# Late steps of a fused attention and expert layer: where products, expert additions, gathers and the turn of c stand

## What is computed

```python
x = L0_attn_x                                    # (8, 512, 512) fp32
xn = layernorm(x)
out = x + attention(xn, Wq, Wk, Wv, Wo) + experts(xn, gate_w, expert_w, expert_b)

def attention(x, Wq, Wk, Wv, Wo):                # 16 heads of 32, causal
    q, k, v = (x @ W.T split into heads for W in (Wq, Wk, Wv))
    q, k = rope(q), rope(k)
    return (softmax(mask(q @ k.T / sqrt(32))) @ v, heads joined) @ Wo.T

def experts(x, gate_w, expert_w, expert_b):      # 8 experts, 2 per token, no capacity limit
    top_vals, top_idx = top_k(x @ gate_w.T, 2)
    w = softmax(top_vals)
    return sum over the two chosen of w * (x @ expert_w[e].T + expert_b[e])
```

## Time and profile before

| | |
|---|---|
| median of 3 runs | 986.21 us (985.04 to 988.06) |
| profiled execution | 989.46 us, span of its instructions 987.7 us |
| TensorE matmuls busy | 919.4 us (93%) |
| VectorE busy | 739.2 us (75%) |
| GpSimd busy | 561.2 us (57%) |
| ScalarE busy | 437.1 us (44%) |
| early steps | about 77 to 430 us |
| experts | about 436 to 651 us |
| late steps | about 651 to 988 us |

### The profile page before, as it was taken

How to read it: one execution, slowest core, us unless ns; L and a number is a source line. 1 busy time by engine, 2 the same in 40 slices (tenths; PEclk the granted TensorE clock), 3 DMA queues, 4 the chain that set the end, 5 groups by cost and what they waited for, 6 DMA issues and landing times.

```text
span 987.7 us, 18755 instructions
## 1 busy us (share of the span) xinstructions
PE 919.4 (93%) x6589; PEld 450.7 (46%) x6589; DVE 739.2 (75%) x1327; ACT 437.1 (44%) x711; POOL 561.2 (57%) x553
## 2 busy tenths in 40 slices
PE   2899898899899999989999999998999999999887
PEld 1344344344354544545555555553444444444333
DVE  7888988798789899954444444467788888788865
ACT  5267867757755443431111221133434454334432
POOL 1545677575675446663333333238877888778741
PEclk9999999999999999999999999999999999999999
DMA  6365678598677443396655555455555564555431
GB/s 242 107 225 183 192 268 312 170 331 288 193 261 287 138 163 127 115 335 193 204 175 176 176 177 171 161 193 171 184 176 182 186 196 140 156 184 175 162 109 54
DMA packets 107963, 188.63 MB, mean 191 GB/s; under 512 B 11872, under 2 KB 65248, under 8 KB 102624
## 3 DMA queue, kind: packets, MB, share of 16 engines
q1 hardware_dynamic: 97072, 152.03, 44.4%
q0 software_dynamic: 10800, 35.40, 12.7%
HBM read 117.13 MB, written 70.25 MB: 190 GB/s over the span
## 4 chain that ended last, share of the span: by engine, by line
PE 65%; DVE 14%; DMA 7%; POOL 5%; ACT 4%; issue 3%; SPq 1%; DVEq 0%; ACTq 0%; POOLq 0%
PE psum L952 19%; PE psum L1037 10%; PE psum L1061 6%; PE psum L1000 5%; PE psum L987 5%; PE psum L1003 4%; PE psum L969 4%; PE psum L1046 4%; PE psum L929 4%; DVE top L1486 4%; DMA c_rows<-c_turn 2%; DMA sum_sb<-x 2%; PE psum L971 2%; ACT pT L764 1%; DMA x_blk<-xn_rows 1%
## 5 line engine op out<-in xcount | busy, mean ns | idle before, releaser
L764 ACT ACTIVATE pT<-psum,factors 128x512 f32<-128x512 f32 (+1 forms) x352 | 218.2, 642 | 247.2 <-PE psum L987 238.2
L1486 DVE TENSOR_REDUCE top<-psum 128x1 f32<-128x384 f32 (+3 forms) x352 | 209.9, 634 | 20.8 <-PE psum L971 19.9
L1037 PE MATMUL psum<-xT,w_att 128*128 128x512 f16 x768 | 196.5, 381 | 6.9 <-DVE xT L1437 4.7
L952 PE MATMUL psum<-w_exp,x_gT 128*128 x852 | 195.3, 379 | 0.6 <-DVE x_gT L1442 0.6
L610 POOL DMA_INDIRECT x_g<-xn_rows,tok_of x71 | 67.3, 948 | 131.8 <-PE psum L929 129.5
L969 PE MATMUL psum<-k_stack,q_stack 96*128 96x384 f16 (+3 forms) x512 | 126.6, 300 | 14.3 <-DVE top L1486 13.2
L987 PE MATMUL psum<-q_stack,k_stack 98*128 98x256 f16 (+3 forms) x512 | 128.4, 303 | 7.4 <-ACT pT L764 4.5
L1442 DVE TENSOR_TENSOR x_gT<-psum,x_gT 128x512 f16<-128x512 f32 x71 | 49.0, 692 | 104.4 <-ACT x_gT L788 85.5
L952 PEld LDWEIGHTS psum<-w_exp,x_gT 128*128 128x128 f16 x852 | 83.3, 98 | 85.6 <-issue 0.9
L788 ACT ACTIVATE x_gT<-psum 128x512 f16<-128x512 f32 x71 | 42.3, 597 | 170.0 <-PE psum L929 167.5
L600 POOL TENSOR_TENSOR o_hl<-o_sb,o_hl 128x512 f16<-128x512 f32 x31 | 36.5, 1177 | 129.9 <-ACT o_hl L778 128.7
(11 more groups left out here) (175 smaller groups left out, 1296.3 us busy)
## 6 DMA issues: line engine op xcount, KB each, us to landing
y_rows<-y_sb SPq DMA_DIRECT2D x71, 256.0 KB
w_in<-w_all SPq DMA_DIRECT2D x12, 1024.0 KB, 11.4
q_stack<-qk_rows SPq DMA_DIRECT2D x96, 128.0 KB
k_stack<-qk_rows SPq DMA_DIRECT2D x96, 128.0 KB
x_in<-x SPq DMA_DIRECT2D x8, 1024.0 KB, 9.5
qk_rows<-q_hl SPq DMA_DIRECT2D x32, 256.0 KB
qk_rows<-k_hl SPq DMA_DIRECT2D x32, 256.0 KB
xn_rows<-x_in SPq DMA_DIRECT2D x8, 1024.0 KB, 5.1
```

Of the source, the lines that this page charges most:

```text
L764: act.activation(p_of(j, h, heads), banks[BANK_T + (NT_ * n + k) % 2][:, 0:W], ACT.Exp, scale=factors[:, 0:1]).then_inc(exp_done, 1)
L952: now = pe.matmul(banks[s % 4], x_gT[s % 4][:, xp * C + c, :], w_exp[:, bass.ds(e, 1), wp, c, :].rearrange("p e d -> p (e d)"), start=n == ...
L1037: now = pe.matmul(bank, w_att[:, what, wp, c, g * P:(g + 1) * P], xT[b % 2][:, xp * C + c, :], start=at_pass == 0, stop=at_pass == 3 * C - 1)
L1486: return dve.tensor_reduce(out=top[:, h:h + heads, i], in_=banks[BANK_S + k % 2][:, 0:heads * W].rearrange("p (h t) -> p h t", h=heads), a ...
```

## The change

Nothing of the arithmetic changes. In early steps only the turn of c does: c_hl becomes the first 32 columns of a zeroed tile of 128 (c_wide), and the whole tile is turned, which writes 128 partitions instead of 32; the copy still takes 32. scores(m, 0) no longer waits for c_copied, only scores(m, 1) does, whose bank the turn uses.

In late steps
- TensorE does all four products of step n in step n+1 behind scores(n+2, 3), and turns c behind shifted_scores(n, 10) instead of ahead of unit 9;
- ScalarE copies c behind exps 9 instead of exps 8, so behind the high part of k; in step 28 the high part of q goes behind exps 6;
- VectorE adds the expert rows of step n (n above 16) between the maxima of units 2 and 3 and normalise_o, instead of at the end of the step; step 16's stay at its end;
- GpSimd in step 16 gathers the second tile of step 16 behind mask 1 instead of ahead of k's rope, and both tiles of step 17 behind mask 3 instead of behind mask 1.

```diff
--- before.py
+++ after.py
@@ -124,7 +124,8 @@
     top = at("top", [P, HG, J], F32)
     c_scale = at("c_scale", [P, HG * J], F32)
     c_f = at("c_f", [P, HG * J], F32)
-    c_hl = at("c_hl", [P, 2, HG * J], F16)
+    c_wide = at("c_wide", [P, P], F16)
+    c_hl = c_wide[:, 0:2 * HG * J].rearrange("p (f r) -> p f r", f=2)
     c_turn = at("c_turn", [2 * HG * J, P], F16)
     rden_few = at("rden_few", [P, S // HD], F32)
     w_att = at("w_att", [P, NQ, 2, C, D], F16)
@@ -637,8 +638,6 @@
                     gather_x(1)
                 if n + 3 < N:
                     low_qk(0, n + 3)
-                if n == N1:
-                    gather_y(late_tiles(N1)[1])
                 if n in (CHOOSE + 2, CHOOSE + 3):
                     mask(n, 1)
                 if n + 3 < N:
@@ -646,8 +645,8 @@
                 if n not in (CHOOSE + 2, CHOOSE + 3):
                     mask(n, 1)
                 if n == N1:
-                    gather_y(late_tiles(n + 1)[0])
-                if n >= N1 and n + 1 < N:
+                    gather_y(late_tiles(N1)[1])
+                elif N1 < n < N - 1:
                     gather_y(late_tiles(n + 1)[1])
                 if n + 3 < N:
                     low_qk(1, n + 3)
@@ -660,6 +659,9 @@
                 mask(n, 3)
                 if n in TURN_AT:
                     low_x(TURN_AT[n], 3)
+                if n == N1:
+                    for w in late_tiles(n + 1):
+                        gather_y(w)
 
             pool.wait_ge(trig_in, 16)
             rope(0, 0)
@@ -810,17 +812,19 @@
                 if n == N1:
                     for u in range(4):
                         act.wait_ge(y_stored[u], 16 * len(range(u, NTILE, 4)))
-                if n + 3 < N:
+                if n + G < N:
                     high_qk(0, n + 3)
                 exps(n, 5)
                 exps(n, 6)
+                if n + G == N:
+                    high_qk(0, n + 3)
                 if n - 1 in JOB_AT:
                     high_w(JOB_AT[n - 1])
                 exps(n, 7)
                 if n + G < N:
                     take_v(n + G, BANK_QV)
                 exps(n, 8)
-                if n + 1 < N:
+                if n < N1:
                     copy_c(n + 1)
                 if n + 3 < N:
                     high_qk(1, n + 3)
@@ -828,6 +832,8 @@
                     high_x(TURN_AT[n], 0)
                     high_x(TURN_AT[n], 1)
                 exps(n, 9)
+                if N1 <= n < N - 1:
+                    copy_c(n + 1)
                 exps(n, 10)
                 if n in TURN_AT:
                     high_x(TURN_AT[n], 2)
@@ -963,7 +969,7 @@
                     pe.wait_ge(k_stacked[u], 48 * (m // 3 + 1))
                 if k >= 2:
                     pe.wait_ge(max_done, NS * m + k - 1)
-                elif m:
+                elif k and m:
                     pe.wait_ge(c_copied, m)
                 for h in range(heads):
                     pe.matmul(bank[:, h * W:(h + 1) * W], q_stack[u][0:ROW_C, h0 + h, i * P:(i + 1) * P], k_stack[u][0:ROW_C, h0 + h, 0:W],
@@ -973,7 +979,7 @@
 
             def turn_c(m):
                 pe.wait_ge(c_made, m + 1)
-                pe.transpose(half(BANK_S + 1)[0:2 * HG * J, 0:P], c_hl[:].rearrange("p f r -> p (f r)"), ident16[:]).then_inc(c_turned, 1)
+                pe.transpose(half(BANK_S + 1)[:, 0:P], c_wide[:], ident16[:]).then_inc(c_turned, 1)
 
             def shifted_scores(n, k):
                 h0, heads, j = T_UNITS[k]
@@ -1096,8 +1102,8 @@
                     free_bank_out(n)
                     spread_max(JOB_AT[n - 1])
                 if n and n != N1:
-                    times_v(n - 1, 2)
-                    times_v(n - 1, 3)
+                    for j in range(0 if n > N1 else 2, J):
+                        times_v(n - 1, j)
                 if n in KEEP_AT:
                     free_bank_out(n)
                     if n - 1 in JOB_AT:
@@ -1189,15 +1195,17 @@
                     if n == G:
                         pe.wait_ge(w_lo_done, 4)
                     project_out(wo[0], BANK_KO, 0, 4)
-                if nxt:
+                if n < N1:
                     turn_c(n + 1)
                 shifted_scores(n, 9)
                 if wo:
                     project_out(wo[0], BANK_KO, 4, 8)
                 shifted_scores(n, 10)
-                if nxt:
+                if n < N1:
                     times_v(n, 0)
                     times_v(n, 1)
+                elif nxt:
+                    turn_c(n + 1)
                 else:
                     times_v_last(0, 1, 2)
                 if wo:
@@ -1561,6 +1569,9 @@
                 if nxt:
                     largest_score(n + 1, 2)
                     largest_score(n + 1, 3)
+                if n > N1:
+                    for w in late_tiles(n):
+                        add_experts(w)
                 if n - 1 in JOB_AT:
                     scale_of(JOB_AT[n - 1])
                 if n == 1:
@@ -1624,9 +1635,10 @@
                     spread_low(1, 0)
                     spread_low(1, 1)
                     experts_of_tiles()
-                for w in late_tiles(n):
+                for w in late_tiles(n) if n == N1 else []:
                     add_experts(w)
 
+            dve.memset(c_wide[:], 0.0)
             own.link(dve.memset(c_scale[:], 2.0 ** -LOG_C))
             for u in range(2):
                 dve.memset(k_stack[u][ROW_C:ROW_C + 2, :, :], -2.0 ** LOG_C).then_inc(ones_made, 1)
```

## The result

The changed kernel takes **993.49 us** (median of 6 runs, 987.81 to 996.95) beside 986.41 (6 runs) for the kernel before: ratio 1.0063, 95% interval 1.0043 to 1.0083. Forecast were 982.4, at most 987.4. It is slower by 7.1 us where 3.8 us less were expected. The other 2.6 are that before's profiled run lay 3 us above its own median and after's 0.5.

A forecast was written before the change was run, and what follows sets the result against it. TensorE's own stream was taken to bound steady late steps, with waits for VectorE in early ones. Terms -0.5 - 4.6 + 2.0 + 1.2 + 1.0 - 1.6 - 1.3 = -3.8 us: 986.21 to about 982.4, range 978.6 to 987.4.

The forecast's parts named there:

- Tile switches: TensorE, late steps: full-width turn saves 0.19 us, one group of products instead of two 0.23, together 0.42 per steady step.
- the steady step: Late steps 18 to 27: 20.8 us becomes about 20.38; with step 17, 0.42 saved in each, -4.6 us.
- rival A: Steady steps: late expert additions or the copy of c give the gain back, 986.9 us; chance 0.22.
- The c_wide tile at nothing: Start of the kernel: the memset of c_wide lies beside the first loads and costs nothing, without cover 0.1 us.
- First late steps: Steps 16 and 17: moved gathers make TensorE stand 5 to 6 us, costing +2.0 and +1.2; bounds -5 and +5.
- the clock: Step 17: a stand of 6 us may bring 3.4 us at half clock, losing 1.7; taken at 0.6, +1.0 us.
- Step 28: q's high part follows exps 6, so TensorE's 1.37 us wait goes; net -1.6 us, between -0.4 and -2.
- steps 29 and 30: Last steps: two switches and the wait for c (0.1 to 0.3) go, -0.65 us each.
- Early steps: Steps 0 to 15: the turn's saving is mostly swallowed by waits for VectorE; 0.5 us gained, between 0 and 2.
- the last step: Step 31 keeps its length; its expert rows go ahead of normalise_o with 1 us to spare.
- C: Steady steps: the second gather lands late, at 5.4 us costing 8.8, so slower at 991 us; chance 0.08.

The follow-up runs named there:

- a3: The kernel before with only the turn of c in full width, all places and waits as before: 986.88 us, ratio 1.0006.
- b1: The changed kernel with c turned in 32 columns again, at the changed place: 991.18 us, ratio 1.0045.
- c4: The changed kernel with VectorE's expert additions of all late steps at the end of the step, as before: 1005.12 us, ratio 1.0187.
- d3: The kernel before with 192 unused bytes per partition behind c_hl, nothing else changed: 990.75 us, ratio 1.0037.
- e1: The changed kernel with c_wide behind all other tiles and 64 bytes left where c_hl was, so other tiles keep their old addresses: 988.19 us, ratio 1.0016.
- c1: The changed kernel with step 16's second tile added in step 17 before normalise_o, and step 17's tiles at its end: 984.91 us, ratio 0.9980.
- e2: c1 with c_wide behind all other tiles, so that every other tile has its address of before: 980.6 us, ratio 0.9945.
- d4: The changed kernel itself measured once more, nothing altered: 993.72 us, ratio 1.0063.
- a4: The kernel before with only GpSimd's gathers moved as the change moves them: 987.39 us, ratio 1.0013.
- e3: The kernel before with 256 unused bytes per partition behind c_hl, nothing else changed: 986.63 us, ratio 1.0006.
- d2: The kernel before with c_wide and the full-width turn up to step 16 alone: 992.46 us, ratio 1.0054.
- d1: c1 with c turned in 32 columns up to step 16, the c_wide tile kept: 987.43 us, ratio 1.0011.
- c2: c1 with products, turn and copy of c of steps 28 to 30 and additions from step 29 as in the kernel before: 987.08 us, ratio 1.0006.

## Why the prediction was wrong, and where it was right

**Tile switches and the steady step: right.** Forecast 20.38 with a saving of 0.42; measured 20.36 and 0.45. The turn alone brought 0.20 to 0.21 (a3, b1; I had taken 0.19). Steps 18 to 27 brought 4.16 of the 4.2 that ten steps of 0.42 are. Copy and additions did fit, if by little: rival A didn't happen, and c4 shows that the experts' place is what pays for it.

**The c_wide tile at nothing: the step that failed.** I priced its memset and its columns, not its bytes. It is the largest term that was missing: 4.0 us by the pad alone (d3), 4.6 by giving the changed kernel the old layout (e1), 3.5 between c1 and e2, and 4.6 on average in the start of the late steps. The +3.62 that the first section left open is this, within what single traces scatter. I had looked only at the engines' instructions; a diff that changes a tile's size in a kernel that places tiles one behind another changes all addresses behind it. The Trainium skill (DMA: Bandwidth & Descriptors, How a descriptor splits into AXI transactions) has the rule that I passed over: a descriptor is split into transactions of 256 bytes that start at multiples of 256, and one that starts between them fetches the bytes ahead of it as well. The page speaks of reading, and the loads here are shifted on the side that is written. Estimates by this rule, in its beats of 32 bytes: a run of 512 bytes that starts 192 past a multiple takes 22 in place of 16, 1.38 times, and the packets of 512 bytes took about 1.27 times as long; a run of 1,024 takes 1.19 times as many, and the packets took 1.05. The 1024 packets of 256 bytes, stores of c_turn, test it the other way: c_turn starts 192 bytes past a multiple before and 128 past one in the shifted kernels, so the rule gives 12 beats in place of 14, 0.86, and they took 17.2 to 17.4 ns in place of 19.2 to 19.4, 0.90. So the trace agrees in direction for three sizes and roughly in size for two of them; it is not the whole account. That 256 bytes of pad cost nothing is what it says.

**First late steps: mechanism right, size short.** On the time scale of the kernel before, whose late steps start 3.62 earlier, TensorE's stand ended at 675.1 where I had 675.3, after 5.98 us where I had 5 to 6. Step 17 cost 1.5 more where I had 0.8 (1.2, less the 0.42 of its switches). The term that was mis-sized is **the clock**: I gave a possible stretch of 3.4 us the weight 0.6 and 1.0 us in all. It was 6.8 us long, in both profiled executions of this kernel (after, d4) and in the three others with a stand of about 6 us (b1, c4, e1), and right on the products: from the end of the stand to shifted_scores(17, 0) 7.86 us passed, where 5.4 were forecast. That is about 2.5 lost. Forecast for the two steps and the clock 3.8, measured 5.8.
What I left unsaid is that the stand needed both moves: a4 moves the gathers alone and steps 16 and 17 come out 0.4 shorter together. And c1 shows that its whole price hung on one tile's addition in VectorE's order: step 16 falls from 29.17 to 20.28.

**Step 28 right in part by luck, steps 29 and 30 wrong by the clock.** Step 28 gained 2.2 (forecast 1.6). But 1.5 of it is a stretch of half clock that the step has in the profile of before (21.71) and in d3 and e3, and not in a3, a4 and d2 (20.20 to 20.26), behind the same wait of 1.36 to 1.37. Steps 29 and 30 were to gain 0.65 each and lost 0.75 and 0.26: each has 3.4 us of half clock behind a stand of 1.57 to 1.92 for the maxima, and I had no term for it. Without the stretch step 30 takes 13.99, in a second profile of the same kernel (d4), and 0.62 less than before, as forecast; so the stretch costs 0.88 there. Step 29 has one in every profile of this order, so that its order and its clock can't be told apart. Before stands as long in these steps, here in step 29, and had no such stretch there, only the one of step 28:

```profile
932.57 0.34 PE L969 MATMUL psum<-k_stack,q_stack 96*128 96x384 f16 x1 [1.57 <-DVE top L1486]
```

So a stand of that length is not enough to foretell it. Nor is the one of 2.82 to 2.85 us for a mask in step 16 of the kernels with the old gathers and products: the clock falls in it or just behind it in a3, d2 and e3, and not in before and d3. What else is needed stays open.

**Early steps: no gain to be seen.** I had -0.5 for the turn. Giving the 32 columns back there made nothing faster (d1 beside c1), and full width there can't be told from the pad alone (d2 beside d3). Kernels with the same early code and addresses differ by several microseconds between the starts of shifted_scores 0 and 15 (351 to 355 in the seven profiles that share the changed kernel's): a single trace can't carry a term of 0.5 there. What does show there, over eighteen profiles, is the layout.

**The sum.** By medians the change costs 7.1 us and I had forecast a gain of 3.8. Of the 10.9 between them the layout is 4.0 to 4.6, steps 29 and 30 are 2.3, the first late steps with the clock 2.0, the last step 0.4, and step 28 gives 0.6 back. That is 8.1 to 8.7. The early gain that didn't come is 0.5 more. The rest, some 2 us, I leave open; it has the size by which the two profiled executions lie differently to their medians (2.6). Without the layout the forecast would have come out near the upper edge of its range, 987.4: e1 took 988.19, with an interval (0.9998 to 1.0034) that holds both sides of it. Of the rivals C had the right sign by a wrong way: the gathers of the steady steps landed in time in every step, and only the one of step 17 took 7.2 us.

## What to carry to other kernels

Before trusting that a new or larger tile costs nothing, look where it stands: put it behind the others, or pad it so that tiles which transfers fill or empty in short runs stay at the multiple of 256 bytes that they had. When work moves off the place where an engine used to be fed during a late transfer, price the two moves together, since one alone may be free (a4); and price a stand of TensorE of several microseconds with the slow stretch that can follow it. If one late transfer holds a queue, adding its data a step later is worth more than hurrying it.

## What was not expected of the hardware

- The alignment of tiles in SBUF shows in transfers: +192 bytes made 12288 packets of 512 bytes take about 48 ns in place of 38 and the kernel 4.0 us (0.37%) longer; +256 bytes made no difference. That this is the splitting of runs fits the packet times of three sizes in direction, that of 256 bytes, which got shorter, among them; it wasn't isolated further, and 128 bytes weren't tried.
- In five of five profiles with a stand of about 6 us the clock fell 1 to 3.3 us before its end and stayed at half for 6.8 us. In step 30 a stretch of 3.4 us cost 0.88 (14.87 and 13.99 in two profiles of the changed kernel), one of 6.8 cost 2.05 (16.66 in c2, 14.61 before). Behind stands of 1.4 to 2.9 us it came or stayed away at the same place of the same code: behind the 1.37 of step 28 in three of six profiles.
- GpSimd's operation on k took 1.27 us alone and 1.74 beside VectorE's additions, and gets the difference back once these are moved. An indirect gather lands in 3.8 us as a rule, and the last one of step 17 took 7.2, issued behind three others within 4 us; the DMA engines' share was 0.94 at 282 GB/s from 677.7 to 684.5.
